# Two attentions on pairs of 64-row tiles, and a square root moved from ScalarE to GpSimd, in a chain of four attentions

## The chip, the cores and the metric

One core of one Trainium2 chip. The metric is the device time of one execution in microseconds (us). The profile is one profiled execution of the same program; its times are given from the start of its span.

## The reference, cut to what matters

Four attention blocks follow each other, for each of 8 batch elements (in one launch):

```python
x = _L0(x, ctx)          # 16 heads of 64, 256 queries x 256 keys, then a layer norm
x = _L1(ctx, x, mask)    # 16 heads of 16, 128 latents (queries), 128 context + 128 latent keys, rms norm, MLP
x = _L2(x, ctx, mask)    # 16 heads of 16, 128 queries x 128 keys, layer norms before and after, MLP
x = _L3(x, mask, ctx, mask)  # 16 heads of 8, 256 queries x 256 keys, mean and spread of the values:
#   mean = attn @ v ; ex2 = attn @ (v*v) ; std = sqrt(relu(ex2 - mean*mean))
#   out  = (masked_instance_norm(x) * std + mean) * mask
```

The second attention is `_L1` and the third `_L2`; the last one's square root is the `std` of `_L3`, 128 x 256 values per batch element (here "a batch").

## The kernel before, in words

**Order of work.** Each engine has one instruction queue written out by hand, batch by batch; semaphores tie them together. `sequences` (L91) lists the order in which the two PSUM banks `MX` (row maxima) and the two banks `SC` (scores) are used. The last attention of batch b is interleaved with the first attention of batch b+1 (`mixed`), the projections of batch b+1 ("fill": `project`, L572 to L580) stand in gaps of the second and third attentions and the MLPs of batch b. Two further PSUM banks `PV` take the sums over values, two `GP` everything else. Weights stay in SBUF except those of the two MLPs, which SP's queue loads again for every batch.

**An attention in this kernel** has a pass for the row maxima (TensorE computes scores from bf16 copies, VectorE reduces them over the keys, L1371, TensorE transposes the negated maxima, L662 and L664) and a pass for the scores (transposed: keys on the partitions). The second pass first adds the shifts (a bf16 matmul with the selection matrix `sel`, L878), then the f32 scores (L880); ScalarE takes the exponential (L1187), TensorE multiplies by the values, which carry ones for the denominator (L894), and VectorE divides (`quotient`: a one-element `gate` instruction L410, a shuffle L1442, a reciprocal L1443, a product L1444). Then TensorE projects the result (`slots_out`, L952).

**Second and third attention before** (`attention`, on PE, ACT and DVE). The head dimension is 16, so 8 heads share the 128 rows of a key tile. Queries are spread out with zeros (`blocks12`, VectorE, L1459: four products of 128x512 with `hmask`), so that one 128-row matmul gives one head. ScalarE casts each group of four heads to bf16 (`cast`, L1110) and copies the transposed maxima (`shift_rows`, L1092). A unit is four heads times 128 keys, 512 columns: 8 units in the second attention (4 groups, 2 key chunks), 4 in the third. The maxima units, scores and value products are interleaved by `order_of_maxima` with a lag of one unit. **First and last attention** already run as pairs of 64-row tiles: partitions 0 to 63 and 64 to 127 hold different heads, two matmuls on the two halves of the rows write two PSUM banks (`maxima_pair3` L624 and L630, `scores3` L771 and L775), and the units come in pairs.

**The end of the last attention**, for batch b-1, runs inside batch b: VectorE `end3` (L1502, and a reciprocal of 128x256, L1504) after the second unit of the second attention; GpSimd `norm3` (L1667 to L1674), then GpSimd `end3` (L1642 to L1646, five 128x256 instructions, the last of them signals `s_v`); then GpSimd's `power(b,1)` (L1659: 128x1 to the power of minus one half, for the norm after the second attention); ScalarE `std3` takes the square root of 128x256 (L1215) after the second attention and then a one-element Exp (L1216), each with an activation table load; GpSimd `output3` (L1651 to L1653) follows and signals `s_o3`, on which SP stores the result. GpSimd's queue goes on with `power(b,2)` (for the norm ahead of the third attention, which VectorE needs at L1496) and `power(b,3)`. After batch 7 the same steps run once more, alone. In GpSimd's queue:

```python
                if not is_first(b):
                    norm3(b - 1)
                    end3(b - 1)
                power(b, 1)
                if not is_first(b):
                    output3(b - 1)

                power(b, 2)
```

VectorE's work of the first MLP is `mlp`: X (L1472), two instructions with both inputs in SBUF per half (L1479 and L1484), after which TensorE computes the second layer (L969), VectorE `x1` (L1563), the statistics (L1491, a gate L410, L1492, L1493), GpSimd `power(b,2)`.

Of the kernel before, what the change touches and what calls it, by code (L numbers as in the profile page):

```python
# [22 lines left out]
BF16 = mybir.dt.bfloat16  # L23
# [5 lines left out]
P = 128  # L29
B = 8  # L30
D = 256
# [21 lines left out]
STEPS = {0: 4, 1: 2, 2: 1, 3: 4}  # L53
LAG = {1: 1, 2: 1}
# [7 lines left out]
UNITS1 = [(1, g, u) for g in range(NG) for u in [*range(STEPS[1]), "T"]]  # L62
UNITS2 = [(2, 0, 0), (2, 1, 0), (2, 0, "T"), (2, 2, 0), (2, 3, 0), (2, 2, "T")]
# [27 lines left out]
def sequences():  # L91
# [3 lines left out]
    def units(b, names):  # L95
        for L, g, u in names:
            b_of = b + 1 if L == 0 else b
            for v in ([u] if u == "T" or L in (1, 2) else ["B0", "B1"] if u == "B" else [u, u + 1]):
                mx.append((b_of, L, g, v))
# [14 lines left out]
    for b in range(B):  # L114
        units(b, UNITS1)
        units(b, UNITS2)
        sc.extend((b, 1, n) for n in range(NG * STEPS[1]))
        sc.extend((b, 2, n) for n in range(NG * STEPS[2]))
# [9 lines left out]
SHIFTS12 = [unit[:3] for unit in MX_SEQ if unit[3] == "T" and unit[1] in (1, 2)]  # L128
SHIFTS03 = [unit[:3] for unit in MX_SEQ if unit[3] == "T" and unit[1] in (0, 3)]
# [33 lines left out]
def build(nc, z_in, ctxT_in, ctx_in, mask1, mask2, mask3, w0, wo, w1qk, w1v, w1o, w1a, w1b,  # L163
          w2qkv, w2o, w2a, w2b, w3, cols_in, rows_in, ident_in, hmask_in, sel_in, out):
    with ExitStack() as stack:
# [31 lines left out]
        hmask = sb("hmask", [P, 8 + 4 + 2 + 128])  # L197
        spread = hmask[:, 14:142].rearrange("p (i c) -> p i c", i=2)
# [9 lines left out]
        Q12 = work[:, 0:NH * P].rearrange("p (h l) -> p h l", l=P)  # L208
# [12 lines left out]
        Qb = sb("Qb", [P, 2, 2 * D], BF16)  # L221
        Q3b = sb("Q3b", [P, 4, D], BF16)
# [3 lines left out]
        nm = sb("nm", [P, 2, 2, HG], BF16)  # L226
# [30 lines left out]
        warm = sb("warm", [P, 1])  # L257
# [23 lines left out]
        def row(name):  # L281
# [14 lines left out]
        mx_done, nmT_ready, nmT03_ready, p_ready, ps_ready = (  # L296
            sem(n) for n in ("mx_done", "nmT_ready", "nmT03_ready", "p_ready", "ps_ready"))
# [3 lines left out]
         s_Qx, s_K1, s_K1b, s_V1, s_K2,  # L301
         s_K2b, s_V2, s_K3, s_K3b, s_v3, s_V3, s_Ax, s_U3) = (sem("s_" + n) for n in (
             "Q0", "Qb", "K0", "V0", "A0", "x0", "x0T", "var0", "pow0", "latT", "lat", "hT", "qs",
             "Qx", "K1", "K1b", "V1", "K2",
# [50 lines left out]
        def mx_bank_taken(n):  # L355
# [4 lines left out]
            if u == "T" and L in (1, 2):  # L360
                return nmT_ready, SHIFTS12.index((b, L, g)) + 1
            if u == "T":
                return nmT03_ready, SHIFTS03.index((b, L, g)) + 1
# [72 lines left out]
        def shifts(b, L, g):  # L436

            if L in (0, 3):
                return nmT03_ready, SHIFTS03.index((b, L, g)) + 1
            return nmT_ready, SHIFTS12.index((b, L, g // 2 * 2 if L == 2 else g)) + 1  # L440

        def unit_heads(L, g, u):

# [1386 lines left out]
```

## Time and profile before

| | us |
|---|---|
| median of 3 runs | 1227.74 (1224.66 to 1230.02) |
| the profiled execution, its own time | 1224.94 |
| its span | 1223.1 |
| TensorE busy | 1044.4 (85%) |
| VectorE busy | 629.3 (51%) |
| ScalarE busy | 511.3 (42%) |
| GpSimd busy | 231.0 (19%) |
| granted TensorE clock, mean | 0.961 of full speed |

From batch to batch the profile repeats: the same instruction of GpSimd (L1673) starts at 234.9, 378.6 and 522.3 us, 143.7 us apart. The page's busy tenths show TensorE near full in all slices but the last three, where the last batch has no projections of a next batch to fill its gaps. A busy share is an average; the timeline of one batch (here the third, about 355 to 499 us) shows which engine waits for which in each stretch.

### The profile page before, as it was taken

Reading aid. Unit: us, or ns where it says so; the run is one execution under the profiler, and the core shown is the slowest. Engines: PE = TensorE matmul, PEld = TensorE weight load, DVE = VectorE, ACT = ScalarE, POOL = GpSimd, SP = SyncE. Lnnn points to the kernel's source line nnn. Section 1 sums busy time; section 2 is a strip of 40 time slices with the busy share of each in tenths; the row PEclk is TensorE's granted clock in tenths of the full one; section 3 lists DMA queues with packets and bytes.
Section 4 is the critical chain, followed back from the end, with each engine's and each line's share of the span. In section 5 each row is a group of like instructions: output and inputs, shape, how many; then the busy total and the mean of one; then the engine's idle time right before and its main releaser. Section 6 shows DMA issues by size and latency. Waiting matters only on the chain.

```text
span 1223.1 us, 20508 instructions
## 1 busy us (share of the span) xinstructions
PE 1044.4 (85%) x7904; PEld 650.1 (53%) x7904; DVE 629.3 (51%) x1263; ACT 511.3 (42%) x993; POOL 231.0 (19%) x355
## 2 busy tenths in 40 slices
PE   7799889988899879997899888998789988987662
PEld 6466554665455654655546654466546556444430
DVE  1444644646536555456545474464654555555541
ACT  1423354344445344443543444443444434533233
POOL 0310012311213012131113102131111301222003
PEclk9899999999999999999999999999999998998787
DMA  9200020020100120002200102001110022000101
GB/s 376 91 1 30 40 93 25 8 74 24 70 31 1 73 83 25 16 2 74 92 17 16 72 3 92 29 3 74 52 50 23 1 73 84 16 16 5 69 1 35
DMA packets 26783, 59.96 MB, mean 49 GB/s; under 512 B 8120, under 2 KB 18752, under 8 KB 21824
## 3 DMA queue, kind: packets, MB, share of 16 engines
q1 hardware_dynamic: 26688, 58.65, 13.2%
q8 instruction: 65, 1.06, 0.4%
q14 instruction: 30, 0.25, 0.1%
HBM read 53.39 MB, written 5.24 MB: 48 GB/s over the span
## 4 chain that ended last, share of the span: by engine, by line
PE 49%; issue 30%; DVE 10%; POOL 8%; ACT 2%; DMA 1%; DVEq 0%; POOLq 0%; SPq 0%; ACTq 0%
DVE nm L1358 7%; PE PV L706 5%; PE SC L689 4%; PE GP L572 4%; PE GP L960 4%; PE GP L574 3%; PE GP L969 3%; PE GP L753 3%; PE GP L792 2%; PE SC L775 2%; PE GP L944 2%; PE MX L624 2%; PE MX L740 2%; PE PV L727 1%; PE MX L609 1%
## 5 line engine op out<-in xcount | busy, mean ns | idle before, releaser
L1358 DVE TENSOR_REDUCE nm<-MX 128x2 bf16<-128x512 f32 x256 | 165.2, 690 | 133.1 <-PE MX L630 81.1
L1157 ACT ACTIVATE Pr<-SC,bcol 128x512 f32<-128x512 f32 x128 | 81.2, 687 | 97.9 <-PE SC L775 97.9
L1685 POOL TENSOR_TENSOR Psum<-Pr 128x512 f32<-128x512 f32 x56 | 70.9, 1267 | 258.9 <-ACT Pr L1155 258.9
L572 PE MATMUL GP<-zP,W 128*128 128x128 f32 x512 | 106.1, 291 | 7.3 <-DMA W<-w 7.3
L1187 ACT ACTIVATE Pr<-SC,bcol 128x512 f32<-128x512 f32 x96 | 66.0, 688 | 102.1 <-PE SC L880 102.1
L1155 ACT ACTIVATE Pr<-SC 128x512 f32<-128x512 f32 x128 | 69.3, 594 | 91.3 <-PE SC L689 91.3
L880 PE MATMUL SC<-work,K 128*128 128x512 f32 x192 | 104.3, 625 | 0.0
L574 PE MATMUL GP<-uP,W 128*128 128x128 f32 x512 | 103.6, 286 | 0.0
L572 PEld LDWEIGHTS GP<-zP,W 128*128 128x128 f32 x512 | 84.1, 203 | 11.0 <-issue 9.3
L574 PEld LDWEIGHTS GP<-uP,W 128*128 128x128 f32 x512 | 82.3, 202 | 0.0
L1659 POOL TENSOR_TENSOR stat<-stat,half 128x1 f32<-128x1 f32 x24 | 13.6, 565 | 344.8 <-DVE stat L1493 270.9
L1371 DVE TENSOR_REDUCE nm<-MX 128x2 bf16<-128x512 f32 (+1 forms) x96 | 63.4, 683 | 28.0 <-PE MX L648 27.4
L960 PEld LDWEIGHTS GP<-oT,WA 128*128 128x128 f32 x512 | 70.8, 222 | 7.0 <-issue 5.3
L960 PE MATMUL GP<-oT,WA 128*128 128x128 f32 x512 | 73.4, 309 | 1.3 <-issue 0.8
L775 PE MATMUL SC<-work,K 64*128 64x512 f32 x256 | 70.1, 605 | 0.0
L706 PE MATMUL PV<-Pr,V 128*64 128x256 f32 x512 | 69.4, 392 | 0.0
L689 PE MATMUL SC<-Q,K 64*128 64x256 f32 x512 | 67.3, 381 | 0.0
L969 PE MATMUL GP<-WB,work 128*128 128x256 f32 x256 | 59.3, 384 | 8.5 <-DVE work L1484 8.5
L1082 ACT ACTIVATE K<-GP 128x512 f32<-128x512 f32 x32 | 19.1, 598 | 109.5 <-PE GP L574 109.5
L1443 DVE RECIPROCAL U<-U 128x128 f32<-128x128 f32 x64 | 61.0, 953 | 2.2
L1110 ACT ACTIVATE Qb<-work 128x512 bf16<-128x512 f32 x64 | 39.8, 630 | 42.4 <-DVE work L1459 33.1
L969 PEld LDWEIGHTS GP<-WB,work 128*128 128x128 f32 x256 | 47.3, 190 | 18.1 <-issue 12.3
(185 smaller groups left out, 1854.2 us busy)
## 6 DMA issues: line engine op xcount, KB each, us to landing
WA<-w1a SPq DMA_DIRECT2D x8, 1024.0 KB, 4.8
WB<-w1b SPq DMA_DIRECT2D x8, 1024.0 KB, 7.0
WA<-w2a SPq DMA_DIRECT2D x8, 1024.0 KB, 4.9
WB<-w2b SPq DMA_DIRECT2D x8, 1024.0 KB, 7.0
W<-w SPq DMA_DIRECT2D x6, 1024.0 KB, 10.2
scratch<-U SPq DMA_DIRECT2D x16, 256.0 KB, 2.0
C<-scratch SPq DMA_DIRECT2D x96, 32.0 KB
zP<-z_in SPq DMA_DIRECT2D x8, 128.0 KB, 2.1
```

The costliest lines, as they stand in the source:

```text
L572: pe.matmul(dst, W0[:, piece, 2 * s, at:at + P], zP[:, s * P:s * P + P], start=True, stop=False)
L574: mm = pe.matmul(dst, W0[:, piece, 2 * s + 1, at:at + P], uP[:, s * P:s * P + P], start=False, stop=True)
L689: mm = pe.matmul(SC[r][:, kc * D:kc * D + D], K0[half, k, kc * P:kc * P + P], Q0[half, k, :], start=False, stop=True, skip_group_check=True)
L706: mm = pe.matmul(bank[64 * j:64 * j + 64, i * D:i * D + D], V0[:, kc, h * 64:h * 64 + 64], Pr[:, (n + j) % 4, kc * D:kc * D + D], start=(k ...
L775: pe.matmul(SC[j][:].rearrange("p (t l) -> p t l", l=D), K3[half, g % 2, kc * P:kc * P + P], Q3[half, g // 2 * 2:g // 2 * 2 + 2, :], start ...
L880: pe.matmul(SC[n % 2][:].rearrange("p (h l) -> p h l", l=w), K(heads[0])[:, kc * P:kc * P + P], Qf(heads[0], len(heads)), start=False, sto ...
L960: mm = pe.matmul(g[:, j * P:j * P + P], WA[:, c, f * P:f * P + P], oT[:, c, :], start=(c == 0), stop=(c == 1), skip_group_check=True)
L969: mm = pe.matmul(g[:, 0:D], G[:, f * P:f * P + P], WB[:, f, :], start=(f == 0), stop=(f == 7))
L1155: act.activation(Pr[:, (n + j) % 4, :], SC[j], ACT.Exp, scale=0.125).then_inc(p_ready, 1)
L1157: act.activation(Pr[:, (n + j) % 4, :], SC[j], ACT.Exp, bias=bcol[:, 3 + k % 2:4 + k % 2], scale=8.0 ** -0.5).then_inc(p_ready, 1)
L1358: dve.tensor_reduce(dst[:, g % 2, :, c:c + 1], MX[(n + i) % 2][:].rearrange("p (a k) -> p a k", a=2), AX_X, ALU.max, negate=True).then_inc ...
L1685: pool.tensor_tensor(Psum[:, c % 4, :].rearrange("p (a l) -> p a l", l=D), two[:, :, 0:D], two[:, :, D:2 * D], ALU.add)\
```

## The change

- Second and third attention (`attention12` in place of `attention`, on PE, ACT and DVE): the queries keep only four masks (`hmask` columns 0 to 3: which 16 of 64 rows), so that a 64-row tile holds four heads at a time and the two halves of the rows are two tiles. Maxima, shifts and scores of two groups are issued in pairs, one per half, into the two banks. 4 pairs in place of 8 units in the second, 2 in place of 4 in the third attention. The value products are as before.
- The masked queries come in two copies: bf16 from VectorE (`Q12b`, two instructions in place of four), f32 from GpSimd (`Q12`, two instructions of 128x512 per attention, new). ScalarE's casts for these attentions are gone, its copies of the transposed maxima go to VectorE; the four transposes of the second attention become two.
- VectorE divides only after all maxima of the attention and `end3(b-1)`, `fill("qp2")` moves behind the maxima.
- The masks `m1row` and `m2row` are loaded to all 128 partitions in place of one.
- `std3` on ScalarE is gone. GpSimd takes the square root as C3[:,1] to the power `plus` (0.5), at the end of its `end3`. In GpSimd's queue `power(b,1)` now stands ahead of `norm3(b-1)` and `end3(b-1)`, and `output3(b-1)` behind `power(b,2)`, `res1` and the f32 queries of the third attention.

```diff
-UNITS1 = [(1, g, u) for g in range(NG) for u in [*range(STEPS[1]), "T"]]
-UNITS2 = [(2, 0, 0), (2, 1, 0), (2, 0, "T"), (2, 2, 0), (2, 3, 0), (2, 2, "T")]
+UNITS1 = [(1, 0, 0), (1, 0, 2), (1, 0, "T"), (1, 1, 0), (1, 1, 2), (1, 1, "T")]
+UNITS2 = [(2, 0, 0), (2, 0, "T"), (2, 1, 0), (2, 1, "T")]
...
+                def maxima_pair12(g, u):
...
+                    for i in range(2):
+                        half = slice(64 * i, 64 * i + 64)
+                        pe.matmul(MX[(n + i) % 2][:].rearrange("p (a k) -> p a k", k=keys), sel[half, 0, :],
+                                  mrow[half, :].unsqueeze(1).to_broadcast([64, per, keys]), start=True, stop=False,
...
                     for j in range(per):
...
+                        for i in range(2):
+                            half = slice(64 * i, 64 * i + 64)
+                            mm = pe.matmul(MX[(n + i) % 2][:, j * keys:j * keys + keys],
+                                           Q12b[half, 4 * g + u // 2 * per + j, :], Kb[half, g, :],
...
+            def attention12(b, L, make, K, V, v_ready, amid=lambda: None):
...
+                    for t in range(4):
+                        for r in range(2):
+                            half = slice(64 * r, 64 * r + 64)
+                            if t == 0:
+                                pe.wait_ge(p_ready, n - 1 + r)
+                            pe.matmul(SC[r][:, t * P:t * P + P], sel[half, 4 * c + t, :], nmT[half, c, :],
+                                      start=(t == 0), stop=False, skip_group_check=True)
+                    for r in range(2):
+                        half = slice(64 * r, 64 * r + 64)
+                        pe.matmul(SC[r][:].rearrange("p (t l) -> p t l", l=P), K[half, c, kc * P:kc * P + P],
+                                  Q12[half, 4 * c:4 * c + 4, :], start=False, stop=True,
...
+                entry, then = (UNITS1[:4], [UNITS1[4:5], UNITS1[5:]]) if L == 1 else (UNITS2[:3], [UNITS2[3:]])
+                for _, g, u in entry:
+                    if (g, u) == (0, "T"):
                         amid()
                     make(g, u)
...
+                for i, (c, kc) in enumerate(steps):
+                    scores(c, kc)
+                    if i == 1:
                         pe.wait_ge(*v_ready)
+                    for _, g, u in (then[i] if i < len(then) else []):
+                        make(g, u)
+                    if i:
+                        pv(*steps[i - 1])
+                pv(*steps[-1])
...
-            def std3(b):
-
-                act.wait_ge(s_v, b + 1)
-                wait(act, st_out, 16 * b)
-                act.activation(C3[:, 3, :], C3[:, 1, :], ACT.Sqrt).then_inc(s_std, 1)
-                act.activation(warm[:], half[:], ACT.Exp)
...
+            def attention12(b, L, amid=lambda: None, after=lambda: None):
+                units = UNITS1 if L == 1 else UNITS2
+                for _, g, u in units:
+                    if (g, u) == (0, "T"):
                         amid()
                     maxima(b, L, g, u)
...
+                after()
+                for g in range(NG):
+                    quotient(b, L, g)
...
                 pool.tensor_scalar(C3[:, 1, :], C3[:, 1, :], 0.0, None, ALU.max).then_inc(s_v, 1)
+                pool.wait_ge(s_v, b + 1)
+                wait(pool, st_out, 16 * b)
+                pool.tensor_tensor(C3[:, 3, :], C3[:, 1, :], plus[:].to_broadcast([P, D]), ALU.pow).then_inc(s_std, 1)
...
+            def blocks12(b, L):
+
+
+                pool.wait_ge(s_qs, 2 * b + L)
+                for c in range(2):
+                    pool.tensor_tensor(Q12[:, 4 * c:4 * c + 4, :],
+                                       qs[:, c * P:c * P + P].unsqueeze(1).to_broadcast([P, 4, P]),
+                                       hmask[:, 0:4].unsqueeze(2).to_broadcast([P, 4, P]), ALU.mult)\
+                        .then_inc(s_Qx, 1)
...
+                blocks12(b, 1)
                 pool.wait_ge(s_lat, b + 1)
                 pool.tensor_tensor(res1[:], lat, row("ob1"), ALU.add).then_inc(s_res1, 1)
                 pool.tensor_tensor(res2[:], lat, row("b2"), ALU.add).then_inc(s_res2, 1)
+                power(b, 1)
                 if not is_first(b):
                     norm3(b - 1)
                     end3(b - 1)
-                power(b, 1)
-                if not is_first(b):
-                    output3(b - 1)
 
                 power(b, 2)
                 pool.wait_ge(s_x1, b + 1)
                 pool.tensor_tensor(res1[:], x1[:], row("cb"), ALU.add).then_inc(s_res1, 1)
+                blocks12(b, 2)
+                if not is_first(b):
+                    output3(b - 1)
```

## Rows read from the trace of the kernel before

**Rows 1.** Page, part 1: busy time and share of the span.

```profile
PE 1044.4 (85%) x7904; PEld 650.1 (53%) x7904; DVE 629.3 (51%) x1263; ACT 511.3 (42%) x993; POOL 231.0 (19%) x355
```

**Rows 2.** Timeline of PE, second attention of the third batch: start, us, instruction.

```profile
368.31 0.38 PE L641 MATMUL MX<-b1row,sel 128*128 128x512 bf16 x1
...
368.74 0.38 PE L641 MATMUL MX<-b1row,sel 128*128 128x512 bf16 x1
...
373.17 0.39 PE L878 MATMUL SC<-nmT,sel 128*128 128x128 bf16 x4
373.39 1.08 PE L880 MATMUL SC<-work,K 128*128 128x512 f32 x2
...
388.35 0.42 PE L894 MATMUL PV<-Pr,V 128*32 128x128 f32 x8 [0.42 <-ACT Pr L1187]
...
390.64 0.70 PE L952 MATMUL GP<-W1O,Ax 128*128 128x256 f32 x2 [0.38 <-DVE Ax L1444]
```

**Rows 3.** Timeline of the last batch: scores of the last attention, two 64-row tiles.

```profile
1192.14 1.02 PE L775 MATMUL SC<-work,K 64*128 64x512 f32 x4
```

**Rows 4.** Groups by line and shape: maxima, exponentials, value products (busy us, mean ns | idle before).

```profile
L1371 DVE TENSOR_REDUCE nm<-MX 128x2 bf16<-128x512 f32 x64 | 42.2, 681 | 19.6 <-PE MX L648 19.1
...
L1187 ACT ACTIVATE Pr<-SC,bcol 128x512 f32<-128x512 f32 x96 | 66.0, 688 | 102.1 <-PE SC L880 102.1
```

**Rows 5.** Timeline of DVE, third attention, third batch: first and last of the quotients.

```profile
422.24 0.16 DVE L410 TENSOR_TENSOR gate<-half 128x1 f32<-128x1 f32 x1 [1.69 <-issue]
...
428.46 0.29 DVE L1444 TENSOR_TENSOR Ax<-PV,U 128x128 f32<-128x128 f32 x1
```

**Rows 6.** Timeline of ACT between second attention and the norm after it.

```profile
388.31 1.28 ACT L1215 ACT_TABLE_LOAD   x1
...
391.84 0.42 ACT L1278 ACTIVATE U<-xa 128x256 f32<-128x256 f32 x1 [0.30 <-DVE xa L1552]
```

**Rows 7.** Groups by line and shape on GpSimd: powers and plain arithmetic (busy us, mean ns).

```profile
L1685 POOL TENSOR_TENSOR Psum<-Pr 128x512 f32<-128x512 f32 x56 | 70.9, 1267 | 258.9 <-ACT Pr L1155 258.9
...
L1659 POOL TENSOR_TENSOR stat<-stat,half 128x1 f32<-128x1 f32 x24 | 13.6, 565 | 344.8 <-DVE stat L1493 270.9 <-DVE stat L1555 73.9
...
L1701 POOL TENSOR_TENSOR stat<-stat,half 128x2 f32<-128x2 f32 x8 | 5.8, 729 | 47.3 <-DVE stat L1534 47.3
...
L1651 POOL TENSOR_TENSOR C<-C,xm 128x256 f32<-128x256 f32 x8 | 5.8, 724 | 1.9 <-ACT C L1215 1.9
```

**Rows 8.** Timeline of POOL, third batch: start of norm3, end of end3, powers 1 and 2.

```profile
376.04 0.19 POOL L1667 TENSOR_TENSOR stat<-stat 128x1 f32<-128x1 f32 x1 [1.10 <-DVE stat L1502]
...
383.68 0.87 POOL L1646 TENSOR_SCALAR C<-C 128x256 f32<-128x256 f32 x1
392.62 0.57 POOL L1659 TENSOR_TENSOR stat<-stat,half 128x1 f32<-128x1 f32 x1 [8.07 <-DVE stat L1555]
...
408.35 0.56 POOL L1659 TENSOR_TENSOR stat<-stat,half 128x1 f32<-128x1 f32 x1 [12.86 <-DVE stat L1493]
```

**Rows 9.** Timelines of POOL and DVE, third batch: a GpSimd instruction beside VectorE's gate.

```profile
379.88 0.72 POOL L1674 TENSOR_TENSOR xm<-xm,m 128x256 f32<-128x256 f32 x1
...
379.90 0.72 DVE L410 TENSOR_TENSOR gate<-half 128x1 f32<-128x1 f32 x1
```

**Rows 10.** Timeline of DVE, third batch: the first MLP's last step.

```profile
402.34 1.29 DVE L1484 SCALAR_TENSOR_TENSOR work<-work 128x512 f32<-128x512 f32 x2 [0.34 <-ACT work L1227]
```

**Rows 11.** Timeline after the last batch: the square root between GpSimd's two parts.

```profile
1215.95 0.87 POOL L1646 TENSOR_SCALAR C<-C 128x256 f32<-128x256 f32 x1
...
1218.68 0.72 POOL L1651 TENSOR_TENSOR C<-C,xm 128x256 f32<-128x256 f32 x1 [1.86 <-ACT C L1215]
```

**Rows 12.** Windows of 1 us: length, busy PE, PEld, DVE, ACT, POOL, granted clock, DMA.

```profile
430.00:431.00 1.00, 0.00 (x0) 0.00 (x0) 0.83 (x4) 0.99 (x2) 0.02 (x1) 1.00 0.00 0
...
435.00:436.00 1.00, 1.00 (x7) 1.00 (x6) 0.88 (x2) 0.00 (x0) 0.00 (x0) 0.50 0.00 0
...
438.00:439.00 1.00, 1.00 (x11) 1.00 (x11) 0.35 (x2) 0.63 (x1) 0.00 (x0) 1.00 0.00 0
```

More of the change, by code:

```diff
@@ L116, in sequences @@
         units(b, UNITS2)
-        sc.extend((b, 1, n) for n in range(NG * STEPS[1]))
-        sc.extend((b, 2, n) for n in range(NG * STEPS[2]))
+        sc.extend((b, 1, n) for n in range(8))
+        sc.extend((b, 2, n) for n in range(4))
         if b < B - 1:
@@ L127 @@
 SC_AT = {unit: n for n, unit in enumerate(SC_SEQ)}
-SHIFTS12 = [unit[:3] for unit in MX_SEQ if unit[3] == "T" and unit[1] in (1, 2)]
-SHIFTS03 = [unit[:3] for unit in MX_SEQ if unit[3] == "T" and unit[1] in (0, 3)]
+SHIFTS = [unit[:3] for unit in MX_SEQ if unit[3] == "T"]
 def reduced(n):
@@ L256, in build @@
         half = sb("half", [P, 1])
[L257 removed]
+        plus = sb("plus", [P, 1])
         m1row = sb("m1row", [P, P], I32)
@@ L900, in attention @@
                         amid()
                     make(g, u)
-                units = [(g, u) for g in range(NG) for u in range(steps)]
-                for n, (g, u) in enumerate(units):
-                    for unit in order_of_maxima(L)[n]:
-                        make(*unit)
-                    scores(g, u)
-                    if n == LAG[L]:
-                        pe.wait_ge(*v_ready)
-                    if n >= LAG[L]:
-                        pv(*units[n - LAG[L]])
-                for unit in units[-LAG[L]:]:
-                    pv(*unit)
+                steps = [(c, kc) for c in range(2) for kc in range(halves)]
@@ L1273, in keys1 @@
                         ins.then_inc(sem_done, 1)
-                attention(b, 1, 1.0 / 16, amid=keys1, filling=latents)
-                if not is_first(b):
-                    std3(b - 1)
+                keys1()
+                latents()
+                attention12(b, 1, 1.0 / 16)
                 act.wait_ge(s_xa, 2 * b + 1)
@@ new lines, in maxima @@
+                if u == "T":
+                    dve.wait_ge(mx_full[n % 2], n // 2 + 1)
+                    if L in (0, 3):
+                        dst, w = (nmT3 if L else nmT0)[:, g % 2, :], D
+                    else:
+                        dst, w = nmT[:, g, :], P
+                    dve.tensor_copy(dst, MX[n % 2][:].bitcast(BF16)[:, 0:w]).then_inc(nmT_ready, 1)
+                    return
+                for i in range(2):
+                    dve.wait_ge(mx_full[(n + i) % 2], (n + i) // 2 + 1)
@@ L1542, in body @@
                 v1("v1", 1)
-                def steps1(n):
-                    if n == 1 and not is_first(b):
-                        end3(b - 1)
-                    if n >= 3 and n % 2:
-                        quotient(b, 1, (n - 3) // 2)
-                attention(b, 1, steps1, lambda: (v1("v1c", 0), fill("qp0")))
-                quotient(b, 1, 3)
+                attention12(b, 1, lambda: (v1("v1c", 0), fill("qp0")),
+                            lambda: None if is_first(b) else end3(b - 1))
                 g = take(o, "o1")
@@ L1571, in body @@
                 blocks12(b, o, 2)
-                attention(b, 2, lambda n: fill("qp2") if n == 1 else None)
-                for g in range(NG):
-                    quotient(b, 2, g)
+                attention12(b, 2, after=lambda: fill("qp2"))
                 g = take(o, "o2")
```

297 lines of the change are left out of this document (99 added, 198 removed).

## The prediction

> **What bounds the kernel now.** I read the page first, then the timelines of one batch engine by engine, then the windows. The page shows TensorE busy for 85% of the span and GpSimd for 19% [rows 1], so TensorE's work looks like the limit and GpSimd like free space. The timelines correct both halves of that. In the second attention TensorE goes from one unit to the next without idle time, so its work is the pace there; at the end of that attention it waits 0.42 us for the last exponential and 0.38 us for the last quotient [rows 2], so there the pace is latency. In the third attention the quotients set the end: from the first gate (422.24) to the last product (428.75) VectorE is busy for 6.5 us, 1.6 us for each of four [rows 5]. And GpSimd, idle as it is, holds a place in the chain: each norm waits for a 0.57 us power in its in-order queue, the first at 392.62, the second at 408.35 [rows 8]. Between the two it has 15.2 us (393.19 to 408.35). What the change puts in there is the main question.
>
> **The attentions on 64-row tiles.** A unit costs TensorE 0.43 us for maxima (368.31 to 368.74), 0.22 us for shifts (373.17 to 373.39) and about 1.0 us for scores [rows 2], 1.65 us together. That two tiles run side by side is seen in the last attention: four instructions of 512 columns take 1.02 us there [rows 3], where two take 1.08 now [rows 2]. So 12 units become 6 pairs and TensorE is relieved of 6 x 1.65 = 10 us per batch, 80 us in all. That is the upper end of the gain. I don't take it, because the two banks of a pair are now filled and emptied together:
> - Entry of the second attention. Two pairs of maxima stand ahead of the filling work, and the second pair needs both banks back: two reductions of 0.68 us [rows 4]. TensorE idles about 1.4 us there, and about 0.9 us for the transposed maxima and the next pair after the filling work. VectorE gains two of its four mask products (0.6 us each in its timeline) and ScalarE the casts, which lets the first pair start no earlier, since the values' projection ends at 368.1. The scores begin about 1.7 us later than at 373.17 [rows 2].
> - The scores. A round is 1.07 us of scores and two exponentials of 0.69 us [rows 4] with the hop, 2.6 us; four rounds and the last value products need 11.3 us where now 15.6 pass (373.17 to 388.77 [rows 2]). Gain 4.3 us.
> - The end. The last two quotients now wait for the last round, where now only one is left: 1.6 us more [rows 5], less 0.36 us because the first half's products end earlier: 1.25 us.
> - Sum for the second attention: 1.7 - 4.3 + 1.25 = -1.3 us.
> - Third attention: the four quotients start after the second round of scores. By the same durations that is at about 422.1 against 422.24 now, and 6.5 us of quotients follow either way [rows 5]. Gain 0.2 us.
>
> I take 1.5 us per batch, 12 us in all. The far ends are a gain of 80 us, and a loss of 2 us per batch (16 us), if every new wait costs the 0.4 us hop more and nothing overlaps.
>
> **GpSimd's f32 queries** are four instructions of 1.27 us per batch [rows 7]. The first two run while it waits for the latents, seven microseconds before the scores need them; the other two stand behind `power(b,2)`, some 2 us of slack. Nothing is charged. If that cover were gone, a third attention would start up to 2.5 us later. The masks' loads and products for 128 partitions in place of one are issued at the same places and run long before they are used; VectorE's copies of maxima (four of 0.3 us) replace ScalarE's six. Nothing for either. `end3` on VectorE (1.9 us) lies ahead of its quotients, in a stretch where it waits for value products.
>
> **The square root.** On ScalarE two table loads and two activations go, 3.2 us per batch (388.31 to 391.5). They end 0.3 us before the next work of ScalarE is released at 391.84 [rows 6], so inside the batches they cost nothing and bring nothing. After the last batch they are on the path, 1.86 us from the end of L1646 (1216.82) to L1651 (1218.68) [rows 11].
>
> What comes is a power of 128x256 on GpSimd, X. No row shows one so wide. The rows have 128x1 at 0.565 us and 128x2, with the same kind of broadcast exponent, at 0.729 us: 0.164 us for one more column [rows 7]. Ordinary arithmetic costs 0.19 us at one column [rows 8] and 0.724 at 256 [rows 7], 2 ns per column. Bounds: X = 1.1 us, if after the start-up of 0.37 us that a power has over plain arithmetic its columns cost what other arithmetic's do; X = 0.565 + 255 x 0.164 = 42.4 us, if each column costs what the second does. I take 42.4, because the only two rows of the operation give it, and both are the same instruction in this kernel. The Trainium skill, GPSIMD Engine Reference, section on elementwise cycle accounting, gives about 2.6 cycles per element for two-input work and names no operation for which it is otherwise; by that X would be an estimated 1.1 us and the time about 1216. The rows of the adds agree with it, those of the powers don't.
>
> **What waits for it.** `power(b,1)` ends at 393.19. Behind it now come norm3 and end3, 8.5 us (376.04 to 384.55 [rows 8]), so the power of 128x256 starts at 401.7 and ends at 444.1. `power(b,2)` stands behind it and would be 35.8 us late (444.1 against 408.35). VectorE is hit earlier. A gate of VectorE with two operands in SBUF, which takes 0.16 us alone [rows 5], took 0.72 us and ended with GpSimd's instruction beside it [rows 9]. L1484, with both operands in SBUF, is due at 402.34 [rows 10], in the first microsecond of the power. If it has to wait for the power's end, the 6.0 us of work from it to `power(b,2)` follow after: the stall is 444.1 - 402.3 = 41.8 us, or X - 0.6. I take that one. The Trainium skill, page SBUF — State Buffer, section Who interferes with whom, has the pair of ports held exclusively for the whole instruction; the trace shows it up to 0.73 us only, and no run here for a power.
>
> Batch 0 has no such step, so the stall comes seven times: 293 us. After about 2 us without work the granted clock went from 1.00 to 0.50 and was full again 3 to 4 us later [rows 12], which costs 1.7 us of work; after each stall I add 2 us, 14 us in all. After the last batch X replaces 1.86 us: +40.6 us.
>
> **Sum.** 1224.9 (the profiled execution's own time, 2.8 below the median of the runs) - 12 + 292.6 + 14 + 40.6 = 1560 us. In general: 1213 + 7 (X - 0.6) + (X - 1.8), and 14 where the stall is long. With X = 2.3 us the change pays for nothing: that is the point from which the power decides.
>
> **Rivals.**
> - A, the forecast, chance 0.55: X above 35 us. Its own range is 1470 to 1620: X = 35 gives 1501, VectorE not held back takes off 7 x 6 = 42, the attentions -24 to +16, the clock up to 5 us a stall.
> - B, chance 0.24: the wide power has a dearer start and cheaper columns than the second one, X between 3 and 35. The narrow rows can't exclude it, because a loop may show its speed only over many columns. At X = 20 it gives 1213 + 136 + 18 + 14 = 1381.
> - C, faster, chance 0.15: X near 1.1, the power is arithmetic like any other. Then 1213 + 3.5 - 0.7 = 1216, and down to 1145 if TensorE's relief of 80 us came through. Against it: a second column of a power costs 80 times a column of an add [rows 7].
> - D, no difference, chance 0.06: X about 2.3, or C with the attentions gaining nothing, because the end of each is set by quotients and exponentials: 1220 to 1232.
>
> **How the numbers follow.** I count within 0.5% (6 us) as the same; a measurement of this kernel can't tell less. Faster 0.15, same 0.06, slower 0.79. The range from 1212 to 1615 holds A, B, D and the better part of C's weight near 1216; it is wide because one unknown price is multiplied by eight. The likeliest case alone is 1470 to 1620.
>
> **What would show it.** In the profile after: an instruction of GpSimd with `plus` of about 42 us, eight times; VectorE's L1484 or the gate behind the second norm waiting until it ends; `power(b,2)` with no idle time before it; TensorE idle for about 40 us ahead of the third attention in seven batches but not in the first; granted clock at half behind it. The batches' distance should be 143.7 - 1.5 + 44 = 186 us, batch 0's about 142. The second attention from its first maxima to its projection should take about 22 us for 23 now, the third the same as now. A power of a few microseconds makes the forecast wrong at once; a power of 42 us with a far smaller stall would mean that something else hides it.

## The result, and the profile after

The changed kernel takes 1544.82 us (median of 4 runs, 1544.74 to 1545.58); the kernel before 1226.38 on the same occasion. The ratio is 1.2593, 95% interval 1.2561 to 1.2625. The forecast was 1560 us, from a reason that came true in its main part: a power of 128x256 on GpSimd costs 41.5 us and stands ahead of a power that a norm waits for. What it had wrong are the hold on VectorE and the tiles' share; the two errors partly cancel.

The page of the changed kernel, its parts 1, 4 and 5 (busy us, share, instructions; the chain that ended last; the costliest group):

```profile
PE 1017.7 (66%) x7888; PEld 641.7 (42%) x7888; DVE 625.9 (41%) x1263; ACT 436.4 (28%) x849; POOL 612.1 (40%) x395
...
PE 42%; POOL 30%; issue 14%; DVE 10%; ACT 3%; DMA 1%; SPq 0%; DVEq 0%; POOLq 0%; ACTq 0%
...
L1564 POOL TENSOR_TENSOR C<-C,plus 128x256 f32<-128x256 f32 x8 | 332.4, 41546 | 0.7
```

Against [rows 1]: TensorE is busy for 27 us less (1044.4 to 1017.7), although its mean granted clock fell from 0.961 to 0.836, and the kernel is 318 us longer. GpSimd went from 19% to 40% busy, which still looks like an engine with room, but it now holds 30% of the chain. The wide power is 332 us of its 612 us of work.

The timeline of GpSimd in the third batch, second attention's norm to the second norm (start, us):

```profile
437.37 0.55 POOL L1587 TENSOR_TENSOR stat<-stat,half 128x1 f32<-128x1 f32 x1 [18.76 <-DVE stat L1472]
...
445.54 1.19 POOL L1561 TENSOR_SCALAR C<-C 128x256 f32<-128x256 f32 x1
446.80 41.62 POOL L1564 TENSOR_TENSOR C<-C,plus 128x256 f32<-128x256 f32 x1
488.41 0.55 POOL L1587 TENSOR_TENSOR stat<-stat,half 128x1 f32<-128x1 f32 x1
```

The last line has no idle time in brackets: the second norm's power starts when the wide one ends, where before GpSimd had waited for its input [rows 8]. VectorE in the same stretch:

```profile
446.72 1.70 DVE L1406 SCALAR_TENSOR_TENSOR work<-work 128x512 f32<-128x512 f32 x2
...
452.19 0.16 DVE L407 TENSOR_TENSOR gate<-half 128x1 f32<-128x1 f32 x1
...
452.48 0.15 DVE L1415 TENSOR_SCALAR stat<-stat 128x1 f32<-128x1 f32 x1
...
488.99 0.80 DVE L1418 TENSOR_SCALAR xb<-x,stat 128x256 f32<-128x256 f32 x1 [34.64 <-POOL stat L1587]
```

This is the part that the forecast had wrong. L1406 (L1484 of before) isn't held until the power's end at 488.42: the first of its two instructions starts 0.08 us before the power, the second starts inside it, at 447.49, and takes 0.92 us in place of 0.69. The gate runs inside the power in its usual 0.16 us. VectorE has the statistics ready at 452.63 and waits only at L1418. The norm's power is 35.8 us late (488.41 against 452.63). That is the forecast's figure without VectorE being held. That it agrees to the tenth is partly luck: the power is 0.8 us shorter than forecast, it starts 0.35 later against `power(b,1)`, and the statistics are ready 0.5 earlier.

To see where all of the time went I took from VectorE's timeline, for each batch, the start of the two query additions (`qs`) and of the two additions after the attentions (`xa`). They cut a batch into four stretches. One batch of the middle (the third), and the batches that differ:

```
us, stretch           second    xa to qs:   third      the rest   whole
                      attention first MLP   attention  (last: end)
before, batch 2       25.79     22.13       16.03      79.81      143.76
changed, batch 2      25.30     58.60       19.57      80.84      184.31
before, batch 0       25.49     21.66       16.03      81.04      144.22
changed, batch 0      26.96     21.65       18.67      80.85      148.13
before, batch 7       25.52     22.96       18.24      69.42      136.14
changed, batch 7      24.14     57.07       19.68     110.05      210.94
all 8 batches, diff.  -2.9     +252.9      +25.4      +43.7      (+0.7 ahead of them: 319.8)
```

319.8 us is the whole difference of the spans (1542.9 less 1223.1). The stall is in the first MLP's stretch, seven times; the last stretch of batch 7, which holds the end, grew by 40.6 us. What the forecast did not have is the third attention: 3.5 us longer, in batch 0, where nothing stalls, 2.6. There the tiles alone are at work, so I looked at them first.

Timeline of VectorE, third attention of the third batch: the query addition and `xa` of before (its first gate is in [rows 5]), then the query addition, first gate and `xa` of the changed kernel:

```profile
413.51 0.42 DVE L1451 TENSOR_TENSOR qs<-GP,cols 128x256 f32<-128x256 f32 x1 [3.20 <-PE GP L944]
...
429.54 0.42 DVE L1577 TENSOR_TENSOR xa<-GP,res 128x256 f32<-128x256 f32 x1 [0.79 <-PE GP L952]
```

```profile
494.74 0.42 DVE L1374 TENSOR_TENSOR qs<-GP,cols 128x256 f32<-128x256 f32 x1 [4.95 <-PE GP L926]
...
506.11 0.16 DVE L407 TENSOR_TENSOR gate<-half 128x1 f32<-128x1 f32 x1 [3.36 <-issue]
...
514.31 0.42 DVE L1492 TENSOR_TENSOR xa<-GP,res 128x256 f32<-128x256 f32 x1 [1.70 <-PE GP L934]
```

Timeline of TensorE in the same attention of the changed kernel:

```profile
499.96 1.71 PE L862 MATMUL SC<-work,K 64*128 64x512 f32 x4
...
507.95 0.66 PE L875 MATMUL PV<-Pr,V 128*32 128x128 f32 x8 [1.54 <-DVE Ax L1367]
...
510.68 3.60 PE L934 MATMUL GP<-W2O,Ax 128*128 128x256 f32 x8
```

and two windows of 2 us there (length, busy PE, PEld, DVE, ACT, POOL, then the granted clock):

```profile
498.00:500.00 2.00, 0.91 (x21) 0.72 (x21) 0.76 (x2) 0.00 (x0) 1.84 (x4) 1.00 0.00 0
...
502.00:504.00 2.00, 1.27 (x10) 0.94 (x12) 0.75 (x2) 0.94 (x2) 0.00 (x0) 0.50 0.00 0
```

TensorE is busy for 0.91 of 2 us, then the granted clock falls to half (1.2 of 2.4 GHz), and the scores that took 1.02 us as a pair [rows 3] take 1.71. VectorE's first gate comes 11.37 us after the query addition (506.11 less 494.74) where it came after 8.73 (422.24 [rows 5] less 413.51), and from the gate to `xa` it is 8.20 us where it was 7.30. 2.64 + 0.90 = 3.54 is the attention's whole growth.

### The profile page after: what moved, and what is told of

It reads as the page before. It is cut to its first block, busy times and chain, and to the rows that moved or that the text cites. A ratio compares the mean times of both kernels' runs of the same rounds, so it can differ in the third digit from the quotient of the medians.

```text
span 1542.9 us, 20302 instructions
## 1 busy us (share of the span) xinstructions
PE 1017.7 (66%) x7888; PEld 641.7 (42%) x7888; DVE 625.9 (41%) x1263; ACT 436.4 (28%) x849; POOL 612.1 (40%) x395
## 4 chain that ended last, share of the span: by engine, by line
PE 42%; POOL 30%; issue 14%; DVE 10%; ACT 3%; DMA 1%; SPq 0%; DVEq 0%; POOLq 0%; ACTq 0%
POOL C L1564 22%; DVE nm L1298 5%; PE PV L684 4%; PE SC L667 3%; PE GP L546 3%; PE GP L548 3%; PE GP L942 3%; PE GP L951 2%; PE GP L731 2%; PE GP L770 2%; PE SC L862 2%; PE SC L753 2%; PE GP L926 2%; POOL work L1579 2%; PE MX L600 1%
## 5 line engine op out<-in xcount | busy, mean ns | idle before, releaser
L1564 POOL TENSOR_TENSOR C<-C,plus 128x256 f32<-128x256 f32 x8 | 332.4, 41546 | 0.7
L1298 DVE TENSOR_REDUCE nm<-MX 128x2 bf16<-128x512 f32 (+1 forms) x352 | 226.9, 688 | 169.4 <-PE MX L606 83.1
L918 PE MATMUL GP<-ident,xb 128*128 128x128 f32 x48 | 13.5, 378 | 280.9 <-DVE xb L1418 274.0
L918 PEld LDWEIGHTS GP<-ident,xb 128*128 128x128 f32 x48 | 5.9, 170 | 292.8 <-issue 292.8
L1124 ACT ACTIVATE Pr<-SC,bcol 128x512 f32<-128x512 f32 x128 | 81.0, 685 | 101.4 <-PE SC L753 101.4
L1418 DVE TENSOR_SCALAR xb<-x,stat 128x256 f32<-128x256 f32 x8 | 6.0, 750 | 242.1 <-POOL stat L1587 242.1
L1151 ACT ACTIVATE Pr<-SC,bcol 128x512 f32<-128x512 f32 x96 | 60.7, 683 | 151.7 <-PE SC L862 151.7
L1178 ACT ACTIVATE oT<-GP,cols 128x128 f32<-128x128 f32 x48 | 17.9, 423 | 287.5 <-PE GP L918 287.5
L1579 POOL TENSOR_TENSOR work<-qs,hmask 128x512 f32<-128x512 f32 x32 | 47.8, 1513 | 67.8 <-DVE qs L1374 67.8
L942 PEld LDWEIGHTS GP<-oT,WA 128*128 128x128 f32 x512 | 67.2, 213 | 7.7 <-issue 7.3
L942 PE MATMUL GP<-oT,WA 128*128 128x128 f32 x512 | 69.5, 298 | 0.8 <-issue 0.8
```

The lines of the kernel that those rows point to most:

```text
L942: mm = pe.matmul(g[:, j * P:j * P + P], WA[:, c, f * P:f * P + P], oT[:, c, :], start=(c == 0), stop=(c == 1), skip_group_check=True)
L1124: act.activation(Pr[:, (n + j) % 4, :], SC[j], ACT.Exp, bias=bcol[:, 3 + k % 2:4 + k % 2], scale=8.0 ** -0.5).then_inc(p_ready, 1)
L1298: dve.tensor_reduce(dst, MX[(n + i) % 2][:].rearrange("p (a k) -> p a k", a=a), AX_X, ALU.max, negate=True).then_inc(mx_done, 1)
L1564: pool.tensor_tensor(C3[:, 3, :], C3[:, 1, :], plus[:].to_broadcast([P, D]), ALU.pow).then_inc(s_std, 1)
L1579: pool.tensor_tensor(Q12[:, 4 * c:4 * c + 4, :], qs[:, c * P:c * P + P].unsqueeze(1).to_broadcast([P, 4, P]), hmask[:, 0:4].unsqueeze(2).t ...
```

## The experiments

**The power alone, on the kernel before.**

```diff
                 pool.tensor_scalar(C3[:, 1, :], C3[:, 1, :], 0.0, None, ALU.max).then_inc(s_v, 1)
+                pool.wait_ge(s_v, b + 1)
+                wait(pool, st_out, 16 * b)
+                pool.tensor_tensor(C3[:, 3, :], C3[:, 1, :], plus[:].to_broadcast([P, D]), ALU.pow).then_inc(s_std, 1)
...
+                power(b, 1)
                 if not is_first(b):
                     norm3(b - 1)
                     end3(b - 1)
-                power(b, 1)
-                if not is_first(b):
-                    output3(b - 1)
 
                 power(b, 2)
```

(`std3` of ScalarE gone, `output3` behind `res1`, as in the change.)

> The power of 128x256 alone, with the changed kernel's order of GpSimd's queue; the attentions are those of before. Theory Q (the power costs its place in GpSimd's queue and nothing else): the second norm's power is late by 8.5 + 41.6 - 15.1 = 35 us in seven batches (245), about 2 us a batch for the lower clock after it (14), 40 at the end: 1525 us. Theory P (VectorE's instructions with two SBUF operands wait for the power's end as well, as forecast): 6 us more per batch, 1565 us. If the tiles were what made the kernel slow, 1230.

Measured: 1517.51 us against 1228.97, ratio 1.2354 (1.2323 to 1.2385). Theory Q within 8 us, theory P off by 47. The group on the page:

```profile
L1639 POOL TENSOR_TENSOR C<-C,plus 128x256 f32<-128x256 f32 x8 | 332.0, 41503 | 0.7
```

Timeline of GpSimd and, below it, VectorE, third batch of this kernel:

```profile
439.74 41.62 POOL L1639 TENSOR_TENSOR C<-C,plus 128x256 f32<-128x256 f32 x1
481.35 0.54 POOL L1652 TENSOR_TENSOR stat<-stat,half 128x1 f32<-128x1 f32 x1
```

```profile
445.13 0.16 DVE L410 TENSOR_TENSOR gate<-half 128x1 f32<-128x1 f32 x1
...
445.42 0.15 DVE L1483 TENSOR_SCALAR stat<-stat 128x1 f32<-128x1 f32 x1
```

The same again: the gate runs in 0.16 us inside the power, and 35.8 us (481.35 less 445.57) pass without work for the chain. By the cut into stretches, the first MLP takes 58.57 us here in batch 2, the third attention 16.03 as before. So the power makes 288 us of the change, and the longer third attention belongs to the tiles. The second attention takes 25.50 us here in place of 25.79, without any tiles: `norm3` and `end3` of GpSimd now stand behind `power(b,1)` and no longer beside VectorE's gates.

**The tiles alone.** The changed kernel with `std3` back on ScalarE and GpSimd's order of before:

```diff
-                power(b, 1)
                 if not is_first(b):
                     norm3(b - 1)
                     end3(b - 1)
+                power(b, 1)
+                if not is_first(b):
+                    output3(b - 1)
 
                 power(b, 2)
...
                 blocks12(b, 2)
-                if not is_first(b):
-                    output3(b - 1)
```

> The two attentions on 64-row tiles alone; square root on ScalarE and GpSimd's order as before. The forecast's theory (latencies as summed, clock unchanged): 1.5 us less per batch, 1213 us. Theory C (TensorE has more gaps, the granted clock falls in the third attention, and the value products of its first pair come later): the batch without a power in the changed kernel was 3.9 us longer than before, so 8 x 3.9 = 31 us more, 1256 us. A theory by which TensorE's work is the pace: 1145 us.

Measured: 1246.45 us against 1228.97, ratio 1.0146 (1.0125 to 1.0168). Slower by 17.5 us; neither the 1213 of the forecast, nor the 1256 taken over from batch 0, nor the 1145 of TensorE's work. Two lines of TensorE's timeline, third batch: scores and first value products of the third attention, at full clock:

```profile
426.02 1.09 PE L862 MATMUL SC<-work,K 64*128 64x512 f32 x4
...
429.69 0.65 PE L875 MATMUL PV<-Pr,V 128*32 128x128 f32 x16
```

and VectorE's first quotient gate:

```profile
430.24 0.16 DVE L407 TENSOR_TENSOR gate<-half 128x1 f32<-128x1 f32 x1 [1.63 <-issue]
```

That gate is 9.45 us after the query addition (420.79), 0.72 later than before, and the attention takes 16.75 us, 0.72 more than 16.03. The scores start earlier against the query addition than before (5.23 us, before 5.78), but TensorE makes the first value products only behind the second scores. In batches 1, 3, 4 and 6 the gate comes after the same 9.44 or 9.45 us and the attention takes 17.3 to 17.5, because its last part takes 7.8 to 8.1 us in place of 7.3; in batch 1 the granted clock is 0.60 and 0.55 there (windows 288 to 292). In batch 0 it takes 18.68. A gap in TensorE's work doesn't by itself bring the half clock: in the third batch TensorE is busy for 0.86 of 2 us at the place where it is 0.91 in the changed kernel, and the clock stays full to the attention's end:

```profile
424.00:426.00 2.00, 0.86 (x19) 0.66 (x21) 0.81 (x2) 0.00 (x0) 1.26 (x3) 1.00 0.00 0
```

In the changed kernel the clock had been at half behind the stall, until about 493; whether that is what tips it, no run separates. The second attention takes 25.99 us in batch 2 (25.79 before); two of its four gates meet GpSimd's `norm3` and `end3` and take 0.43 and 0.54 us in place of 0.16. TensorE's busy time fell by 53 us here (1044.4 to 991.0), so much of the relief that was summed is real (80 was the bound); none of it reaches the end.

**Value products ahead of the next scores**, third attention only:

```diff
-                    if i == 1:
+                    if i == (L == 1):
                         pe.wait_ge(*v_ready)
...
-                    if i:
+                    if L == 2:
+                        pv(c, kc)
+                    elif i:
                         pv(*steps[i - 1])
-                pv(*steps[-1])
+                if L == 1:
+                    pv(*steps[-1])
```

> As the tiles alone, but in the third attention TensorE makes the value products of the first pair ahead of the second pair's scores. If the four quotients of VectorE, which start with the first value products, set the end there: 1.2 us less per batch, 10 us less than the tiles alone (about 1246 where that is 1256). If the scores and exponentials set it: no difference or a few us more.

Measured: 1228.53 us, ratio 1.0001 (0.9986 to 1.0015): 18 us less than the tiles alone, more than the 10 expected; by the stretches the third attention gives 15 us of it. TensorE and then VectorE in the third batch:

```profile
425.69 0.43 PE L875 MATMUL PV<-Pr,V 128*32 128x128 f32 x8
426.27 0.43 PE L875 MATMUL PV<-Pr,V 128*32 128x128 f32 x8 [0.15 <-ACT Pr L1154]
426.62 0.40 PE L858 MATMUL SC<-nmT,sel 64*128 64x128 bf16 x8
```

```profile
426.34 0.15 DVE L407 TENSOR_TENSOR gate<-half 128x1 f32<-128x1 f32 x1
```

The gate is now 7.73 us after the query addition (418.61) and the attention takes 15.01 us: 1.7 less than the tiles alone, 1.0 less than before. The quotients set the end of this attention in all three kernels: the first gate at 8.73, 9.45 and 7.73 goes with 16.03, 16.75 and 15.01 us, 7.3 us from gate to `xa` each time (third batch). With this order the tiles cost nothing any more, and gain nothing either: over all eight batches the third attention is 6.0 us shorter than before, but the second is 2.9 longer, the first MLP 1.9 and the rest 4.6. For the rest of a batch I did not find out why by an experiment; TensorE's granted clock is 0.942 on average against 0.961.

**TensorE kept busy in its gaps**, on the tiles alone and on the changed kernel. Four matmuls per batch whose result nobody reads, three of 512 columns and one of 256 (the expectations below say six; the code issues four, and the trace has 64 records of them in all, two for each f32 matmul):

```diff
+                def keep(width, n):
+
+                    if L == 2:
+                        for _ in range(n):
+                            pe.matmul(GP[order_of(b).at("o2")[0]][:, 0:width], ident[:], W0[:, 0, 0, 0:width],
+                                      start=True, stop=True, skip_group_check=True)
...
                     if (g, u) == (0, "T"):
                         amid()
+                        keep(512, 1)
...
+                    keep(256, i == 0)
...
                     for r in range(2):
+                        keep(512, c)
```

> The tiles alone, with six extra f32 matmuls per batch (into a PSUM bank that is free there) in TensorE's gaps of the third attention. In the tiles alone that attention took 16.7 us in batches with the clock at full speed throughout and 18.7 where it fell to half. If the clock is what separates them: 16.7 to 17 us in every batch, 3 to 10 us less in all than the tiles alone (1246.5). If it is the tiles' own waits: no gain, and up to 1 us per batch more for the extra work.

> The changed kernel with the same extra matmuls. Its third attention takes 19.6 us in each batch behind a stall, 2.8 more than the tiles alone at full clock. If that is the half clock: 17 us where the extra work keeps it up, 15 to 20 us less than 1544.8. If the extra work does not keep it up: the same or a few us more.

Measured: the tiles alone 1242.49 us (before 1225.15; ratio 1.0132, 1.0107 to 1.0158, which overlaps 1.0146 of the tiles alone, so the gain as a time is not shown), but the third attention takes 16.75 us in batch 0 too, where it took 18.68, and 16.74 to 17.00 in batches 1 to 6. The changed kernel went from 1544.82 to 1524.34 (two runs, 1519.48 and 1529.19): its third attention takes 16.74 or 16.75 us in six of eight batches in place of 19.57. Two windows of it in the third batch, as far from the query addition (486.81) as those of the changed kernel above, with the granted clock behind POOL's busy time:

```profile
490.00:492.00 2.00, 1.06 (x20) 0.65 (x21) 0.82 (x3) 0.00 (x0) 1.84 (x4) 1.00 0.00 0
...
494.00:496.00 2.00, 1.76 (x24) 0.87 (x28) 0.67 (x2) 0.65 (x2) 0.00 (x0) 1.00 0.00 0
```

More work for TensorE made the kernel 20 us faster. The 2.8 us that separate the third attention of the changed kernel from that of the tiles alone at full clock (19.57 and 16.75) are the half clock. Batch 0 is weaker evidence: its second attention, which stands ahead of all extra matmuls, also took 25.3 us in both of these kernels where it takes 26.96 without them, so there the clock differed before the extra work began.

**The power at another place.** In the changed kernel it moves out of `end3` and behind the second norm's power, the residual and the third attention's f32 queries (after the last batch it stays between `end3` and `output3`):

```diff
                 blocks12(b, 2)
                 if not is_first(b):
+                    root(b - 1)
                     output3(b - 1)
```

> The changed kernel with the power of 128x256 moved behind the second norm's power, the residual and the third attention's queries, so that the third norm's power waits for it. If the stall is the power less what GpSimd would have idled there: the first MLP is back at 22.1 us, the third attention with its norm is 41.6 + 3.5 - 18 = 27 us late, against 36.4 before; 7 x 9.4 = 66 us less, 1479 us. If the power costs its full 41.6 us wherever it stands: 1545. If it hides behind the longer work there: 1290.

Measured: 1478.88 us (1475.34 and 1482.41), the first theory's 1479. The first MLP is back at 21.75 us, and the rest of a batch, which now holds the stall ahead of the third norm, takes 108 to 112. The rest of a batch is 28.5 us longer on average in batches 1 to 6, against 27 expected. So at the two places tried, the cost is the power less what GpSimd would have idled there. The agreement of the total is closer than that of its parts: the third attention was expected unchanged and gave 6.6 us in all.

**The power in four pieces**, on the kernel before (ScalarE keeps the last batch's root, with nothing beside it to hide a power):

```diff
                     end3(b - 1)
+                    root(b - 1, 0)
                 power(b, 1)
                 if not is_first(b):
-                    output3(b - 1)
+                    root(b - 1, 1)
 
                 power(b, 2)
                 pool.wait_ge(s_x1, b + 1)
                 pool.tensor_tensor(res1[:], x1[:], row("cb"), ALU.add).then_inc(s_res1, 1)
+                if not is_first(b):
+                    root(b - 1, 2)
+                power(b, 3)
+                pool.tensor_tensor(res2[:], xa[:], row("pb"), ALU.add).then_inc(s_res2, 1)
+                if not is_first(b):
+                    root(b - 1, 3)
+                    output3(b - 1)
                 apart.wait((s_o3, b))
                 pool.tensor_scalar(m3[:], m3row[:], 0.0, None, ALU.add).then_inc(s_msk, 1)
-                power(b, 3)
-                pool.tensor_tensor(res2[:], xa[:], row("pb"), ALU.add).then_inc(s_res2, 1)
```

> The kernel before, with ScalarE's square root replaced (but for the last batch's) by four powers of 32, 72, 104 and 48 columns, put where GpSimd idles. Theory Q and a linear price of 0.164 us per column: pieces of 5.4, 11.9, 17.1 and 8 us, all within GpSimd's idle time, 1225 to 1230 us. Theory P (a power holds VectorE's two-operand instructions until it ends): gates and L1484 wait in three places, 3 to 5 us each, 1300 us. If the wide power is cheaper per column than a narrow one, the pieces show it: their durations do not lie on one line through the 41.6 us of 256.

Measured: 1225.11 us (10 runs) against 1228.97, ratio 0.9971 (0.9954 to 0.9987). The groups by shape:

```profile
L1652 POOL TENSOR_TENSOR C<-C,plus 128x104 f32<-128x104 f32 x7 | 118.8, 16967 | 0.0
L1652 POOL TENSOR_TENSOR C<-C,plus 128x72 f32<-128x72 f32 x7 | 83.0, 11862 | 0.0
...
L1652 POOL TENSOR_TENSOR C<-C,plus 128x48 f32<-128x48 f32 x7 | 56.4, 8062 | 0.0
L1652 POOL TENSOR_TENSOR C<-C,plus 128x32 f32<-128x32 f32 x7 | 38.2, 5451 | 0.6
...
L1557 DVE TENSOR_SCALAR xb<-xa,stat 128x256 f32<-128x256 f32 x8 | 3.0, 380 | 5.3 <-POOL stat L1666 5.3
```

From 32 to 104 columns: (16.967 - 5.451) / 72 = 0.160 us per column, and 5.451 + 224 x 0.160 = 41.3 for 256, where 41.5 was measured. The price is linear from one column to 256. 296 us more of GpSimd's time cost nothing, and the kernel is a little faster than before: the scaling L1557, which met `output3` in seven batches before and took 0.81 us there (753 ns on average), takes 380 ns beside a power. That is 0.4 us for each first MLP (21.68 us against 22.13), 3.8 us over the eight stretches. The medians show a gain of 3.9 us; the kernel before had a median of 1225.15 on another occasion, so the reason to believe in the gain is the stretch.

This kernel also answers the forecast's question about VectorE more cleanly than the changed one. Both steps of the first MLP with two SBUF inputs (L1479 and L1484 of before) run there with a power around them. GpSimd, then VectorE, third batch:

```profile
392.43 11.86 POOL L1652 TENSOR_TENSOR C<-C,plus 128x72 f32<-128x72 f32 x1
```

```profile
399.38 1.47 DVE L1478 SCALAR_TENSOR_TENSOR work<-work 128x512 f32<-128x512 f32 x2
401.20 1.29 DVE L1483 SCALAR_TENSOR_TENSOR work<-work 128x512 f32<-128x512 f32 x2 [0.34 <-ACT work L1228]
```

1.47 and 1.29 us are what the same steps take before, with nothing on GpSimd (1.29 in [rows 10]). Theory P is excluded for this pair of operations.

**Both reliefs together**: value products ahead, and powers of 32, 80, 72 and 72 columns.

```diff
+                at = (0, 32, 112, 184, 256)
...
                 blocks12(b, 2)
                 if not is_first(b):
+                    root(b - 1, 2)
```

> Tiles with the value products ahead (1228.5 alone) and the square root as four powers of 32, 80, 72 and 72 columns in GpSimd's idle times (1225.1 on the kernel before, where VectorE's scaling ahead of the first MLP no longer met an instruction of GpSimd: 0.45 us less per batch). If the two add up: 1224 to 1226 us, 0.3% less than before. If GpSimd has now too little room (its queries for the tiles take 6 us per batch): a power is late in one of the norms and the time is 1230 to 1250.

Measured: 1237.13 us against 1225.15, ratio 1.0098 (1.0072 to 1.0123). They don't add up; the second expectation came, 1230 to 1250. GpSimd and VectorE in the third batch:

```profile
393.87 5.45 POOL L1580 TENSOR_TENSOR C<-C,plus 128x32 f32<-128x32 f32 x1
399.29 0.55 POOL L1604 TENSOR_TENSOR stat<-stat,half 128x1 f32<-128x1 f32 x1
```

```profile
397.78 0.15 DVE L1484 TENSOR_SCALAR stat<-stat 128x1 f32<-128x1 f32 x1 [0.57 <-ACT U L1225]
```

On tiles VectorE's part of the ending comes after all maxima, GpSimd's `norm3` starts later against the attention's end, and the first piece ends at 399.3; the first norm's sum was ready at 397.9. That is 1.36 us late, and the first MLP takes 22.92 to 24.64 us in batches 1 to 7 in place of 22.12 to 23.14 with the value products ahead alone, 8 us more in all. A smaller first piece was not tried. Of the versions run, only the kernel before with the spread powers is ahead of both kernels, by 0.3%.

## Why the prediction was right, and where not

- **The price of the wide power** was forecast as 0.565 + 255 x 0.164 = 42.4 us and is 41.5. The slope from the two narrow rows [rows 7] held over 256 columns; case B (dear start, cheap columns) and case C fall. The rule of the Trainium skill, GPSIMD Engine Reference, section Elementwise — side-by-side cycle accounting, about 2.6 cycles per element for two inputs, does not hold for this operation: 0.160 us per column, against 0.002 for plain arithmetic in this case [rows 7, rows 8].
- **Seven stalls.** Forecast 41.8 us each, of which 35.8 for the queue and 6.0 because VectorE would be held. The queue's part is what came, 35.8 in the third batch. The step of the mechanism that failed is "L1484, with both operands in SBUF ... If it has to wait for the power's end", 42 us in all. The row it rested on [rows 9] showed a gate beside a multiplication of GpSimd; it was carried over to another operation. The rule of the Trainium skill, page SBUF — State Buffer, section Who interferes with whom, which supported the step with a hold for the whole instruction, is not borne out by a power: two-operand instructions of VectorE ran inside one in the changed kernel, with the power alone and with the power in pieces, most of them in their usual time. Why a power differs from a multiplication stays open.
- **The third attention** was forecast as 0.2 us shorter and became 3.5 longer behind a stall, 2.6 in batch 0, 25 us in all. Right was that the quotients set its end. Wrong was when they start: the first value products stand behind the second scores, which need both exponentials and, as measured, come 0.72 us later at full clock; and the clock was assumed unchanged. The last attention's pairs have work of another attention in their gaps, the third's have none. The sign that would have shown it first is batch 0, which has no stall: forecast 142 us, measured 148.1 (144.2 before).
- **The second attention** was forecast 1.3 us shorter. In the middle batches of the changed kernel it is 0.5 shorter, but 0.3 of that comes with the power alone; the tiles alone make it 0.2 longer. In batch 0 it lost 1.5, with the granted clock at 0.50 in part of it (windows 84 to 86 of the tiles alone). The tiles in all: 17.5 us slower by the experiment, against 12 faster in the sum.
- **The clock after a stall**: 14 us were set aside, and it cost more, about 22. In the first MLP's stretch `power(b,2)` starts 35.3 us later than before, counted from `xa` (35.8 less 0.4 that VectorE's scaling gained), and from it to the query addition pass 6.33 us in place of 5.16: 0.4 of that is L1418, which takes 0.80 us beside GpSimd's residual addition, some 0.8 goes with the half clock, 5 us in seven batches. The other 17 are the 2.8 us of the third attention, above, in batches 1 to 6.
- **GpSimd's f32 queries** were charged nothing, rightly: the two take 2.99 us in place of 2.54, and end at 498.24 where TensorE starts the shifts at 499.74.
- **The end**: 40.6 us forecast, 40.6 measured (110.05 less 69.42). This is luck: from GpSimd's last step of `end3` to `output3` pass 41.3 us in place of 1.86, 39.5 more, and the remaining 1.1 lies elsewhere in the stretch; the tiles alone lengthen it by 1.8 (71.23).
- **The sum**: 335 us forecast and 319.8 found, because the first MLP's stretch came 54 us shorter than its two terms (42 for VectorE, the rest mainly the clock, which cost its time in the third attention instead), and the third attention gave 27 more, the second 7 more and the remaining stretches 4 more than the sum had. The total is nearer than its terms.
- **Rival C** rested on a cheap power and fell with it. That the power can cost nothing after all, in pieces, has another reason, which no rival named: GpSimd's idle time.

The parts don't add exactly. The power alone costs 288.5 us and the tiles alone 17.5; together they cost 318. Of the 12 missing, 2.6 lie between the two medians of the kernel before (1228.97 and 1226.38). In the stretches of the profiles the third attention has 16 us more than the two parts together, since with tiles it meets the lower clock in all batches behind a stall, and the other stretches have 10 less. With the gaps filled, 1524 us is left.

## What to carry to other kernels

Price an operation by its own rows: two narrow instances of a power gave the cost of the wide one to 2%, where any rule for arithmetic would have been off by a factor of forty. An engine at 19% busy has room only between the instructions that others wait for; count the idle time at the place, and split what is put there so that each piece fits. Pairing matmuls on two row tiles gained nothing here, where quotients set the end; whether it pays where other work fills TensorE's gaps, no run here shows. Where an exponential or a quotient sets the pace, first look at which result that engine gets first, since here the order of two steps on TensorE was worth as much as the pairing had cost.

## What the runs showed of the hardware that was not expected

- A power on GpSimd (41.6 us for 128x256) did not hold VectorE's instructions with two SBUF operands (0.16 us for the gate inside it; 1.29 us for L1483 inside a narrower power), while a multiplication on GpSimd did (0.72 us for the gate [rows 9]), and a scaling of 128x256 on VectorE took 0.38 us beside a power and 0.81 beside GpSimd's multiplication. Beside the plain arithmetic of `end3` on GpSimd, in the changed kernel, VectorE's L1401 (L1479 of before, two SBUF inputs) took 1.99 us in place of 1.47, and GpSimd's L1561 1.19 in place of 0.87.
- Two f32 products with masks and a broadcast operand on GpSimd took 2.99 us together, 1.5 us each, where an addition of the same size takes 1.27 [rows 7]; VectorE's two products beside them (bf16 output) took 2.14 us where two of before (f32 output) take 1.25.
- Four extra matmuls per batch made the changed kernel 20 us faster; the granted clock stayed at 2.4 GHz in its third attention.
